# Three stage heads of a two-layer perceiver kernel put in another order on one core

## The reference

```python
x = x + L0_attn(layernorm(x))      # RWKV block: time mix, then channel mix
    h = layernorm(x); hh = time_shift(h)
    k, v, r = (h * tm + hh * (1 - tm)) @ W.T          # three mixes
    x = x + (sigmoid(r) * wkv(k, v)) @ Wo.T           # a scan over the 32 steps
    ... the channel mix: Wck, relu squared, Wcv, gate Wcr
x = x + L0_ffn(layernorm(x))       # softmax over 8 experts, top 2, all experts computed
x = x + L1_attn(layernorm(x))      # Mamba block
    xz = x @ in_proj.T; a causal convolution of 4 taps, silu; a scan; out_proj
```

## Time and profile before

| what | value |
|---|---|
| median of 3 runs | 1822.67 us (1822.65 to 1823.44) |
| the profiled execution | 1822.25 us, span 1820.5 us |
| TensorE matmul, busy | 1365.0 us (75% of the span) |
| VectorE, busy | 1292.3 us (71%) |
| ScalarE, busy | 1009.8 us (55%) |
| GpSimd, busy | 763.9 us (42%) |
| mean granted TensorE clock | 0.84 of 2.4 GHz |

### The profile page before, as it was taken

One profiled execution on the slowest core, in us unless ns is written; L12 is line 12 of the kernel. 1 busy time (PEld: TensorE's weight loads), 2 busy tenths in 40 slices (PEclk: granted clock), 3 DMA queues, 4 the chain that ended last, 5 costly groups with the idle time before them and its releaser, 6 DMA issues. The chain is left out here.

```text
span 1820.5 us, 33510 instructions
## 1 busy us (share of the span) xinstructions
PE 1365.0 (75%) x12580; PEld 769.6 (42%) x12580; DVE 1292.3 (71%) x2324; ACT 1009.8 (55%) x1839; POOL 763.9 (42%) x808
## 2 busy tenths in 40 slices
PE   6998347988479878778836853444688799789898
PEld 4544123656444355555523320001245345445566
DVE  3698899961468765777657428999999899985200
ACT  2676325433444376777653343333598798886553
POOL 2355000000222434434404004666688788777433
PEclk8999668989679878878976975556699899989999
DMA  6496100000145577777511338898665375551000
GB/s 255 162 357 254 67 0 0 1 1 0 66 140 170 166 133 118 122 134 129 79 34 71 95 109 207 188 226 205 161 154 138 93 175 128 127 131 33 1 12 12
DMA packets 152100, 211.84 MB, mean 116 GB/s; under 512 B 107039, under 2 KB 112095, under 8 KB 138880
## 3 DMA queue, kind: packets, MB, share of 16 engines
q1 hardware_dynamic: 151940, 209.70, 45.2%
HBM read 154.85 MB, written 31.75 MB: 103 GB/s over the span
## 5 line engine op out<-in xcount | busy, mean ns | idle before, releaser
L2734 POOL TENSOR_TENSOR mf_st<-mf_st,mf_c_rep 128x1024 f32<-128x1024 f32 x128 | 301.0, 2352 | 226.8 <-DVE mf_st L2802 226.6
L2802 DVE TENSOR_TENSOR_SCAN mf_st<-mf_dA,mf_u_ps 128x512 f32<-128x512 f32 x256 | 310.5, 1213 | 0.0
L2637 PE MATMUL mf_y_ps<-mf_st,c_consts 128*32 128x512 f32 x512 | 143.8, 769 | 150.8 <-POOL mf_st L2734 109.9
L2913 ACT ACTIVATE mf_dA<-c_dt,c_neg_a 128x496 f32<-128x496 f32 x256 | 166.5, 701 | 103.5 <-DVE mf_st L2802 102.6
L2678 PE MATMUL mf_eh<-mf_parts,mf_w 128*128 128x512 f16 x768 | 194.8, 391 | 29.3 <-POOL mf_parts L2753 20.5
L2698 PE MATMUL mf_ey<-mf_w,mf_hid 128*128 128x256 f16 x1536 | 192.8, 277 | 0.0
L2796 DVE TENSOR_TENSOR mf_u_ps<-mf_st,mf_b_ps 128x512 f32<-128x512 f32 x256 | 177.7, 695 | 18.3 <-DMA mf_st<-xs 7.2
L2757 POOL TENSOR_TENSOR mf_hid<-mf_g,mf_hid 128x512 f16<-128x512 f32 x128 | 148.9, 1164 | 96.4 <-ACT mf_g L2930 96.2
L2698 PEld LDWEIGHTS mf_ey<-mf_w,mf_hid 128*128 128x128 f16 x1536 | 152.5, 99 | 49.7 <-issue 5.3
L2927 ACT ACTIVATE mf_hid<-mf_eh,c_vecs 128x512 f16<-128x512 f32 x128 | 87.9, 687 | 124.7 <-PE mf_eh L2678 124.3
L259 POOL TENSOR_TENSOR c_parts<-mg_ln_hT,c_parts 128x512 f16<-128x512 f32 x8 | 9.8, 1255 | 311.8 <-ACT c_parts L250 311.8
(11 more groups left out here) (502 smaller groups left out, 2756.3 us busy)
## 6 DMA issues: line engine op xcount, KB each, us to landing
mf_st<-xs SPq DMA_DIRECT2D x64, 1024.0 KB, 7.3
a_ctx_t<-in_ctx_t SPq DMA_DIRECT2D x16, 1024.0 KB, 9.3
a_ctx_n<-in_ctx_n SPq DMA_DIRECT2D x16, 1024.0 KB, 8.1
cqs<-a_whole_rows SPq DMA_DIRECT2D x16, 512.0 KB, 6.8
mo_raw<-in_l_w SPq DMA_DIRECT2D x16, 512.0 KB, 4.0
ws<-mo_split SPq DMA_DIRECT2D x32, 256.0 KB, 2.6
c_cq<-cqs SPq DMA_DIRECT2D x16, 512.0 KB, 5.9
mf_w<-ws SPq DMA_DIRECT2D x32, 256.0 KB, 9.5
```

Of the source, the lines that this page charges most:

```text
L2637: m = e.matmul(y_ps[T * j:T * j + T, :], c.pick[:, gg, :], st[u % RING][:, j, :], start=(gg == 0), stop=(gg == 3))
L2734: e.tensor_tensor(half(u, h), half(u, h), over(c_rep[u // UNITS % 2][:, :], [P, 2, BT], 1), ALU.mult).then_inc(hcs("done"), 1)
L2802: e.tensor_tensor_scan(st[u % RING][:, j, :], dA[:, n % AHEAD, :], u_ps[j % 2][:, :], 0.0, ALU.mult, ALU.add).then_inc(hs("done"), 1)
L2913: e.activation(by_batch(dA[:, n % AHEAD, :])[:, :, 1:], dt, ACT.Exp, scale=c.neg_a[:, at:at + 1]).then_inc(dAs("done"), 1)
```

## The change

It has four parts in three stages.

In `l0_mixes` the three wide weights signal a semaphore of their own, `wide_in`. TensorE transposes the first block without waiting for weights, waits for the first four weights ahead of the first linear product, and for the wide three in turn 1. VectorE's constants become a function that is called after the first statistics.

In `l0_gates` the root is put ahead of ScalarE's four passes over the expert weights.

In `l1_inner` each of GpSimd's additions to the norms waits for the last norm of all 16, where it waited for the last of its own block.

```diff
@@ l0_mixes, sync
-            e.dma_start(wck[:, :, :], c.d["l0_wck"]).then_inc(loaded, 16)
-            e.dma_start(wcr[:, :, :], c.d["l0_wcr"]).then_inc(loaded, 16)
-            e.dma_start(wcv[:, :, :], c.d["l0_wcv"]).then_inc(loaded, 16)
+            e.dma_start(wck[:, :, :], c.d["l0_wck"]).then_inc(wide_in, 16)
+            e.dma_start(wcr[:, :, :], c.d["l0_wcr"]).then_inc(wide_in, 16)
+            e.dma_start(wcv[:, :, :], c.d["l0_wcv"]).then_inc(wide_in, 16)
@@ l0_mixes, tensor
-            e.wait_ge(loaded, 16 * 7)
             for i in range(-1, BLOCKS + 2):
                 if some(i + 1):
                     turn("turn", i + 1, xn, front, f_turn)
+                if i == -1:
+                    e.wait_ge(loaded, 16 * 4)
+                if i == 1:
+                    e.wait_ge(wide_in, 16 * 3)
                 if some(i - 2):
@@ l0_mixes, vector
-            for k in "kvr":
-                e.tensor_scalar(tm[k][:, :], c.vec[f"tm_{k}"], 1.0, None, ALU.subtract).then_inc(made, 1)
...
-            e.wait_ge(made, 14)
+            def constants():
+                for k in "kvr":
+                    e.tensor_scalar(tm[k][:, :], c.vec[f"tm_{k}"], 1.0, None, ALU.subtract).then_inc(made, 1)
...
+                e.wait_ge(made, 14)
...
             for each in (front, wkv, xi, chan, close):
                 each.start(e)
             front_stats(0)
+            constants()
@@ l0_gates, scalar
             A.start(e)
+            ln_scalar_std(e, V, A, n, 0, c)
             for j in range(CJ):
                 e.wait_ge(w_loaded[j], 16)
...
-            ln_scalar_std(e, V, A, n, 0, c)
             all_scalar(e, T_, A, n, c.parts)
@@ l1_inner, gpsimd
             for i in range(BLOCKS):
                 at = slice(i * KT_, (i + 1) * KT_)
-                e.wait_ge(*N.at("norm", 0, i * KT_ + KT_ - 1))
+                e.wait_ge(*N.at("norm", 0))
                 e.tensor_tensor(res[:, at, :], n.xn[:, at, :], over(c.row["out_b"], [P, KT_, C], 1), ALU.add).then_inc(resid("done"), 1)
```

More of the change, by code:

```diff
@@ L779, in l0_mixes @@
         banks = [ps(f"ps{u}") for u in range(8)]
-        loaded, made = sem("loaded"), sem("made")
+        loaded, wide_in, made = sem("loaded"), sem("wide_in"), sem("made")
         def steps(name, names):
@@ L901, in _ @@
         def _(e):
-            for k in "kvr":
-                e.tensor_scalar(tm[k][:, :], c.vec[f"tm_{k}"], 1.0, None, ALU.subtract).then_inc(made, 1)
[L904 to L917, removed]
-            e.wait_ge(made, 14)
+            def constants():
+                for k in "kvr":
+                    e.tensor_scalar(tm[k][:, :], c.vec[f"tm_{k}"], 1.0, None, ALU.subtract).then_inc(made, 1)
+                for k in "kr":
+                    e.tensor_scalar(cm[k][:, :], c.vec[f"cm_{k}"], 1.0, None, ALU.subtract).then_inc(made, 1)
+                e.wait_ge(made, 6)
+                e.tensor_scalar(wcol[:, :], wcol[:, :], -1.0, None, ALU.mult).then_inc(made, 1)
+                e.memset(decay[:, :], 0.0).then_inc(made, 1)
+                e.memset(pp[:, 0:1], FAR).then_inc(made, 1)
+                e.memset(aa[:, 0:1], 0.0).then_inc(made, 1)
+                e.memset(bb[:, 0:1], 0.0).then_inc(made, 1)
+                e.wait_ge(made, 11)
+                for j in range(CJ):
+                    e.tensor_scalar(decay[:, j * BT:(j + 1) * BT], decay[:, j * BT:(j + 1) * BT], wcol[:, j:j + 1], None,
+                                    ALU.add).then_inc(made, 1)
+                e.wait_ge(made, 13)
+                e.memset(by_batch(decay[:, :])[:, :, 0:1], FAR).then_inc(made, 1)
+                e.wait_ge(made, 14)
             pp_now, pp_was, aa_was, bb_was = pp[:, 1:1 + N], pp[:, 0:N], aa[:, 0:N], bb[:, 0:N]
```

## The result

The changed kernel takes 1811.56 us in the median of 12 executions, the kernel before 1822.11 in as many. The ratio is 0.9941 with a 95% interval of 0.9912 to 0.9969, that is 10.7 us less, 5.6 to 16.0. The forecast was 1811.4. Executions scatter more than the three of before had shown, from 1811.2 to 1828.7 before and from 1796.4 to 1816.3 after, so the stages have to be compared one by one.

What follows compares the result with a forecast made beforehand. No one engine bounds the kernel: stages follow behind barriers, and the edited heads are single chains. Terms 3.5 + 5.0 + 1.5 + 1.3 = 11.3 off 1822.25 give 1810.95, or 1811.4 beside the 0.4 higher median; range 1806.5 to 1816.

Steps and rivals of the forecast that it cites:

- The weights' wait: Head of l0_mixes: transposes need only norms, statistics run ahead of constants, TensorE starts earlier; 3.5 us, ends 2.9 and 3.6.
- The root: Head of l0_gates: root ahead of ScalarE's weight passes brings the first feature copy 4.0 us earlier; 5.0 in all, ends 4.6 and 5.3.
- The logits: End of l0_gates: with TensorE's idling gone, logit records may run at the high clock; 1.5 us, from between 0 and 3.3.
- The third edit: l1_inner: projection 4.1 us earlier, but GpSimd's adds hold the first convolution; 1.3 us left, bounds 4.2 and -1.9.
- a train: l1_inner: GpSimd's eight adds in a row behind the norms, 19.1 us long, ending near 992, holding first-convolution instructions.
- the adds end every 2.39 us: l1_inner: adds end at this spacing (19.1 / 8) from 975.1 to 991.8, one held VectorE instruction getting through per add.
- A: l1_inner: the convolution is not held much; third term 4.2 or 5.5, total 14 to 15.5, 1807.5 us; chance 0.15.
- B: l1_inner: third edit becomes a loss of 1 to 1.9 by falling clock or blocked VectorE, logits stay low; 1815.5; chance 0.14.
- C: All edited stages: starts move but something later sets each end, so no change; 1820 to 1824 us; chance 0.04.
- D: Last stage and those between: clock's high and low stretches fall anew, making the kernel slower; 1827 us; chance 0.03.

Runs made afterwards that it cites:

- spare matmuls: Changed kernel plus three float32 matmuls into a spare bank on TensorE after the first block's transposes in the gates; ratio 0.9930 against the kernel before.
- late rows: Changed kernel with GpSimd's four adds to c.X put behind the whole first convolution, the four to the norms unmoved; ratio 0.9881 against before, median 1801.79 us.
- all adds late: Changed kernel with all eight of GpSimd's adds put behind the whole first convolution in the inner stage; ratio 0.9914 against before, median 1810.34 us.
- the changed kernel again: The changed kernel measured a second time with no edit; ratio 0.9905 against the kernel before, 17.3 us less.

## Why the prediction was right

**The weights' wait, 3.5.** Right. The head gives 3.6 to 3.7 (transposes at 7.96 for 11.65, products at 13.83 for 17.43), and the norms stood at 186.1 on the clock of before, where I had 186.3. The stage gives 4.05, the mean of the four traces in which TensorE waits for all seven weights (288.83) less that of nine with both halves (284.78). What is over comes from the weights: in these four traces the transposes start at 11.65, 11.76, 12.74 and 12.99, 4.3 later in the mean than with both halves, and before's trace was at the short end. The clock is no part of it: the 1.5 us of the changed kernel's first products did not come again in the eight others, where the first eight records take 6.1 to 6.5 up to the next product, with 6.4 before. The split of the term was right too: 2.9 forecast for the norms no earlier than before, 2.9 measured at the transposes, and nothing in the stage for the constants alone. Whether the kernel gets these 4 us when this is the only edit stays open: two measurements gave 1.0003 and 0.9992, and no trace shows a stage that gives them back.

**The root, 5.0.** Right: 4.3 at the first feature copy where I had 4.0, and at the first logit 5.2 in five traces (21.43 to 21.49 behind the first DMA for 26.65), against ends of 4.6 and 5.3. In the changed kernel's own profile it is 5.55, above the upper end, as the last transposes ran at the high clock.

**The logits, 1.5.** The mechanism was right and the size too small. In the changed kernel's own profile they gave 1.7, but in the five others with this edit and no spare matmuls 3.0 to 3.1 (13.66 less 10.58 to 10.65), near my upper end of 3.3. I took the middle between 0 and 3.3 for want of a reason. In all six the clock was high when the logits started, and in five it had risen within 0.1 us of the first; that the blocks before them now follow without a gap may be why, and is not shown. The stage's gain is 7.5 in the mean (52.06 over six traces, 44.57 over six), where I had 6.5.

**The third edit, 1.3.** The mechanism was right, with 0.4 in place of 1.3 at block 0's `rows`. It came as written: norms of 5.25, projection 5.5 earlier (I had 4.1, or 5 with the clock, and 7 to 8 us of transposes that took 6.46), a train, six held instructions, TensorE waiting for `mi_sz`, block 1's fourth product tied to its gate copy. The step that was mis-sized is that "the adds end every 2.39 us". Adds alone take 2.36 (9.45 for four). Adds that VectorE's instructions wait for take 2.70 in the mean (10.81 for four), so the train lasted 20.2 us and not 19.1, and the sixth instruction got through 1.1 us later than worked out. The late rows show that this train alone cost the start of block 0's `rows` 7.2 us, and the stage some 6 in the means. The Trainium skill, "SBUF — State Buffer", section "Who interferes with whom", has the rule that a VectorE instruction with two SBUF inputs and a GpSimd instruction that reads SBUF exclude each other, and that the shared ports are held for a whole instruction; the trace agrees, with 8.24 us for three multiply-adds that take 2.33 when GpSimd is silent.

**The sum.** The means of the two stages and block 0's `rows` in the third give 4.05 + 7.5 + 0.4 = 12.0. The two measurements of the changed kernel are 10.7 and 17.3 less than before, each with 5 to 6 us on both sides. That 1811.4 met 1811.56 owes something to luck: a third term 0.9 too high made up for a gates' gain 1.0 too low, the first term was 0.5 too low, and the clock in stages that were not edited moves a single execution by several microseconds.

**The rivals.** A and B fell with the inner stage's times: the convolution was held, and the fourth product was not later than before. B's clock did fall behind the wait, for 3.4 us, but it was high again when the fourth product started, which had to wait for its gate copy in any case. C fell on the gates, D on all.

## What to carry to other kernels

Moving GpSimd's adds out from between VectorE's instructions is no gain by itself: ask where the train lands, and what stands behind the instructions that it then holds. Here one more wait, that puts half of the train behind the first convolution, turned 0.4 us into 7.6 at block 0's `rows`, some 6 in the whole stage. When a reordering touches several stages, compare each stage from its own first instruction, and up to a point that the edit sets: the mixes repeated within 1.4 us and block 0's `rows` within 1 in one order, where the inner stage as a whole went from 132.9 to 137.7 and whole executions scattered by 20.

## What the runs showed of the hardware

An add of 128 x 1024 on GpSimd took 2.36 us alone and 2.6 to 2.7 in the means of four where VectorE had instructions waiting, so the holding costs both sides. Sixty-four products of 8 columns took 13.3 us from first to last start, 11.6, 10.2 or 9.3, by how much of them met the high clock, and the clock fell in their midst although TensorE was busy throughout. In the inner stage the distance from block 0's `rows` to block 1's was 22.1 us at a mean clock of 1.00, 22.2 to 22.5 at 0.92 and 23.6 to 23.9 at 0.86, over the 13 traces other than that with all adds late. The attention, which no edit touched, took 324 to 338 us: 329 us at a mean clock of 0.83 and 337 at 0.81 in the windows of two traces:

```profile
614.00:943.00 329.00, 242.10 (x6974) 161.60 (x6972) 220.23 (x535) 224.00 (x486) 121.10 (x332) 0.83 0.60 105
```

```profile
613.00:950.00 337.00, 249.21 (x6968) 166.45 (x6968) 217.71 (x530) 223.88 (x486) 121.49 (x332) 0.81 0.58 102
```

The first is the changed kernel again, the second the one with all adds late. TensorE is busy 7 us longer at the lower clock, for the same work. What decides in which execution the clock is lower I did not find out.
